# A decoder layer on one core: last-stage weights fetched in quarters, and three instruction orders changed around the attention heads and the last norm

## The reference

```python
x = x + attn(layernorm(x))                       # one head of width 128, Wqkv, Wo, biases
x = x + xattn(layernorm(x), ctx, mask, pos_bias) # 32 heads of width 128, with an RMS norm inside
x = x + ffn(layernorm(x))                        # below
# xattn, for each of 32 heads and 8 sequences
score = softmax(where(mask, h_q @ h_k.T + pos_bias, -inf)); attn = score @ h_v; out = attn @ w_out.T
# ffn
base = x @ base_W.T; probs = softmax(x @ router_W.T)            # 8 experts, the top 2 of them
mid = (x @ lora_A) * gates; out = base + 2 * (mid @ lora_B)     # rank 16 each
```

## Time and profile before

| what | value |
| --- | --- |
| median of 3 runs | 852.9 us (852.66 to 852.99) |
| the profiled execution, its own time | 854.52 us |
| span of its records | 852.8 us |
| granted clock of PE | 1.00 over the span |
| PE busy | 835.5 us, 98% |
| DVE busy | 643.3 us, 75% |
| ACT, POOL busy | 412.0 us and 361.7 us |

### The profile page before, as it was taken

One profiled execution on the slowest core, in us unless ns is written; L12 is line 12 of the kernel. 1 busy time (PEld: TensorE's weight loads), 2 busy tenths in 40 slices (PEclk: granted clock), 3 DMA queues, 4 the chain that ended last, 5 costly groups with the idle time before them and its releaser, 6 DMA issues.

```text
span 852.8 us, 14086 instructions
## 1 busy us (share of the span) xinstructions
PE 835.5 (98%) x4288; PEld 705.7 (83%) x4288; DVE 643.3 (75%) x1114; ACT 412.0 (48%) x1070; POOL 361.7 (42%) x332
## 2 busy tenths in 40 slices
PE   5999999999999999999999999999999999999998
PEld 4788888888778888878888888888888888888896
DVE  6988877788887876769867887778667876687754
ACT  3934445655554344365544555355534554454320
POOL 2413424324552333255466556553555455644000
PEclk9999999999999999999999999999999999999999
DMA  8026577657665568737966666576657675773002
GB/s 295 14 99 172 149 170 171 153 154 171 168 185 148 148 169 147 160 120 208 251 205 203 196 192 189 183 220 202 183 177 222 176 203 178 203 199 72 1 1 99
DMA packets 231282, 139.79 MB, mean 164 GB/s; under 512 B 139216, under 2 KB 205904, under 8 KB 229328
## 3 DMA queue, kind: packets, MB, share of 16 engines
q1 hardware_dynamic: 231248, 139.38, 60.2%
HBM read 90.07 MB, written 49.28 MB: 163 GB/s over the span
## 4 chain that ended last, share of the span: by engine, by line
PE 88%; DVE 5%; DMA 3%; ACT 1%; POOL 1%; SPq 1%; issue 1%; DVEq 0%; POOLq 0%
PE bank L654 73%; PE bank L714 7%; PE bank L805 6%; DMA values<-turned 1%; DMA by_blocks<-probs 1%; SPq L356 1%; DVE turned L1525 1%; PE bank L677 1%; DVE acc L1298 1%; DVE stats L1305 1%; DVE xt_lo L1353 0%; DMA acc<-in_x 0%; DMA probs_t<-by_blocks 0%; ACT w_hi L1077 0%; DVE acc L1785 0%
## 5 line engine op out<-in xcount | busy, mean ns | idle before, releaser
L1085 ACT COPY st<-bank 128x512 f32<-128x512 f32 x192 | 112.6, 586 | 227.1 <-PE bank L654 226.2
L654 PE MATMUL bank<-ctx_hi,w_hi 128*128 128x512 f32 x448 | 176.8, 395 | 0.9 <-ACT st L1085 0.5
L1431 DVE TENSOR_TENSOR st<-bank,st 128x512 f32<-128x512 f32 x144 | 99.5, 691 | 101.3 <-PE bank L654 96.8
L654 PE MATMUL bank<-ctx_hi,w_lo 128*128 128x512 f32 x448 | 174.5, 390 | 0.0
L654 PE MATMUL bank<-ctx_lo,w_hi 128*128 128x512 f32 x448 | 174.5, 389 | 0.0
L539 POOL TENSOR_TENSOR w_sum<-raw 128x256 f32<-128x256 f32 x48 | 40.1, 836 | 228.1 <-PE bank L654 197.2
L607 POOL TENSOR_TENSOR weighed<-probs,row_scale 128x512 f32<-128x512 f32 x60 | 65.7, 1100 | 118.7 <-DVE row_scale L1383 118.1
L654 PEld LDWEIGHTS bank<-ctx_hi,w_hi 128*128 128x128 f32 x448 | 84.1, 188 | 22.9 <-ACT st L1085 4.4
L654 PEld LDWEIGHTS bank<-ctx_hi,w_lo 128*128 128x128 f32 x448 | 84.1, 188 | 17.7
L654 PEld LDWEIGHTS bank<-ctx_lo,w_hi 128*128 128x128 f32 x448 | 84.2, 188 | 16.7
L1026 ACT ACTIVATE probs<-probs,neg_max 128x128 f32<-128x128 f32 x248 | 96.1, 391 | 0.1
(11 more groups left out here) (153 smaller groups left out, 1514.1 us busy)
## 6 DMA issues: line engine op xcount, KB each, us to landing
raw<-in_weights SPq DMA_DIRECT2D x128, 256.0 KB, 3.4
values<-turned SPq DMA_DIRECT2D x64, 256.0 KB, 4.4
v<-values SPq DMA_DIRECT2D x64, 256.0 KB, 4.8
by_blocks<-probs SPq DMA_DIRECT2D x30, 512.0 KB, 3.2
probs_t<-by_blocks SPq DMA_DIRECT2D x120, 128.0 KB, 2.8
keys<-st SPq DMA_DIRECT2D x14, 1024.0 KB, 4.8
st<-keys SPq DMA_DIRECT2D x28, 512.0 KB, 5.5
acc<-in_x SPq DMA_DIRECT2D x8, 256.0 KB, 6.3
```

What stands on the lines that cost most here:

```text
L654: ins = pe.matmul(out_ap, lhs[a], rhs[b], start=start and k == 0, stop=stop and k == n - 1, skip_group_check=again)
L1085: act.copy(to[:, i, j, :], (y, other, y, y)[which][:, :]).then_inc(act_took, 1)
L1431: dve.tensor_tensor(to[:, i, j, :], (other, y, other)[which][:, :], to[:, i, j, :], ALU.add).then_inc(dve_took, 1)
```

## The change

Four edits. The last stage's weights are fetched in quarters, each at the end of one of the first four `refill` calls, which are written out instead of one; `high_ffn` waits for the count of its own quarter. The two turns of the first head's blocks on DVE stand before the first two `take` calls of K1 instead of behind them. The last head's two halves of values are weighed together, before the output of blocks 0 to 3. The last norm's first half is made in two steps of two blocks: DVE adds, statistics and spreads, POOL roots, ACT and DVE normalisation are interleaved anew, and PE turns rows two blocks at a time (`turn_last_rows`), with a wait for blocks 4 and 5 ahead of chunk 2; of the splits on DVE the first stands ahead of the adds of blocks 6 and 7. `routed(0)` no longer waits for all adds.

```diff
@@ -453,13 +453,16 @@
             fetch_bias(2)
             sp.wait_ge(k_stored, 16 * (GROUPS - 2))
 
-            def fetch_ffn():
-                n = 0
+            def fetch_ffn(i):
+
+                quarter, n = ffn_cols // FFN_PARTS, 0
                 for src, width in ((w_base, KC * C), (w_routed, KC * ROUTED), (w_lora_b, C)):
-                    sp.dma_start(ffn_raw[:, n:n + width], src).then_inc(ffn_loaded, 16)
+                    lo, hi = max(n, quarter * i), min(n + width, quarter * (i + 1))
+                    if lo < hi:
+                        sp.dma_start(ffn_raw[:, lo:hi], src[:, lo - n:hi - n]).then_inc(ffn_loaded, 16)
                     n += width
 
-            def refill(g, first=False, ahead=2):
+            def refill(g, ffn_part=None, ahead=2):
 
                 load_keys(g + 1, 0)
                 sp.wait_ge(pv_done, 2 * PAIR * g + 2)
@@ -474,11 +477,12 @@
                 next_out(g + 1)
                 if ahead == 2:
                     fetch_bias(g + 2)
-                if first:
-                    fetch_ffn()
-
-            refill(1, first=True)
-            with sp.Fori(2, GROUPS - 2) as g:
+                if ffn_part is not None:
+                    fetch_ffn(ffn_part)
+
+            for g in range(1, 1 + FFN_PARTS):
+                refill(g, g - 1)
+            with sp.Fori(1 + FFN_PARTS, GROUPS - 2) as g:
                 refill(g)
             refill(GROUPS - 2, ahead=1)
 
@@ -640,8 +644,9 @@
             with pool.Fori(3 + FFN_PARTS, GROUPS - 1) as g:
                 pair(g)
             pair(GROUPS - 1, last=True)
-            root(2, half(0), spans(2, 0))
-            root(2, half(1), spans(2, 1))
+            root(2, slice(0, 2), 6)
+            root(2, slice(2, HALF), 7)
+            root(2, half(1), 8)
 
 
         @block.tensor
@@ -656,18 +661,29 @@
                         k += 1
                 return ins
 
+            def turn_last_rows():
+
+                for k in range(2):
+                    pe.wait_ge(rows_ready, 6 + k)
+                    pe.wait_ge(rows_ready_v, 2 + k)
+                    for c in range(KC):
+                        if k == 0 and c in (0, 2):
+
+                            pe.wait_ge(out_added, B * GROUPS + 4 + c)
+                        for b in (2 * k, 2 * k + 1):
+                            ins = pe.transpose(ROWS_T[2][c][:, cols(b)], rows[:, b, cols(c)], ident[:, :])
+                        if k == 1:
+                            ins.then_inc(rows_t_done, 1)
+
             def turn_rows(layer, i):
                 if i == 0 and layer:
-                    pe.wait_ge(out_added, (0, B, B * (GROUPS + 1) - HALF)[layer])
-                pe.wait_ge(rows_ready, spans(layer, i))
+                    pe.wait_ge(out_added, B)
+                pe.wait_ge(rows_ready, spans(layer, i) + (layer == 2))
                 if layer == 2:
-                    pe.wait_ge(rows_ready_v, i + 2)
+                    pe.wait_ge(rows_ready_v, 4)
                 elif layer == 0:
                     pe.wait_ge(rows_ready_v, 1)
                 for c in range(KC):
-                    if layer == 2 and i == 0 and c == 2:
-
-                        pe.wait_ge(out_added, B * (GROUPS + 1) - 2)
                     if i:
                         if layer == 1:
                             pe.wait_ge(x_rows_copied, c + 1)
@@ -920,20 +936,16 @@
 
                 turn_last_probs(1)
                 weigh_head_values(g, 0, last=True)
-                weigh_head_values(g, 1, (0,), last=True)
+                weigh_head_values(g, 1, last=True)
                 pe.wait_ge(wo_lo_ready, GROUPS)
                 pe.wait_ge(out_added, B * g + 6)
                 pe.wait_ge(scores_biased, 2 * HEADS + 2)
                 pe.wait_ge(ot_lo_ready, 2 * HEADS - 1)
                 for b in range(HALF):
-                    if b == 3:
-
-                        pe.wait_ge(probs_t1_copied, 1 + PAIR)
                     part(b, 0)
                 pe.wait_ge(ot_lo_ready, 2 * HEADS + 1)
                 for b in range(HALF):
                     part(b, 1).then_inc(out_done, 1)
-                weigh_head_values(g, 1, (1,), last=True)
                 for b in range(HALF, B):
                     if b >= 6:
                         pe.wait_ge(out_added, B * GROUPS + b - 6 + 1)
@@ -979,10 +991,10 @@
                     three_pass(BASE[t][:, :], [([s[:, 0, cols(b)] for s in ot], lora_b_s)],
                                start=False).then_inc(ffn_done, 1)
 
-            turn_rows(2, 0)
+            turn_last_rows()
             pe.wait_ge(ffn_lo_ready, FFN_PARTS)
+            routed(0)
             pe.wait_ge(out_added, B * (GROUPS + 1))
-            routed(0)
             base_out(0, (0,))
             turn_rows(2, 1)
             base_out(0, (1, 2, 3))
@@ -1011,8 +1023,8 @@
                     act.activation(tok_raw[OF_X][:, slot, c % 2, :], ROWS_T[1][c][:, :], ACT.Copy,
                                    scale=ln_w_cols[:, c:c + 1]).then_inc(x_rows_copied, 1)
 
-            def normalise(layer, i, some, last=True):
-                act.wait_ge(rstd_ready, spans(layer, i))
+            def normalise(layer, i, some, last=True, ready=None):
+                act.wait_ge(rstd_ready, ready or spans(layer, i))
                 for b in some:
                     scale = rstd_rms[:, b:b + 1] if layer == 1 else rstd[:, 0, b:b + 1]
                     ins = act.activation(rows[:, b, :], acc[:, b, :], ACT.Identity, scale=scale, bias=shift[:, b:b + 1])
@@ -1254,7 +1266,7 @@
                     then()
 
             def high_ffn(i):
-                act.wait_ge(ffn_loaded, 48)
+                act.wait_ge(ffn_loaded, 16 * (1, 2, 4, 6)[i])
                 at = cols(i, ffn_cols // FFN_PARTS)
                 act.copy(ffn[0][:, at], ffn_raw[:, at]).then_inc(ffn_hi_ready, 1)
 
@@ -1272,7 +1284,8 @@
             copy_last_probs(1)
             split_head_out(GROUPS - 1, 0)
             split_head_out(GROUPS - 1, 1, VO)
-            normalise(2, 0, (0, 1))
+            normalise(2, 0, (0,), ready=6)
+            normalise(2, 0, (2,), ready=7)
 
             def split_last_rows(i):
                 for c in range(KC):
@@ -1281,7 +1294,7 @@
                                    scale=1.0).then_inc(xt_hi_ready, 1)
 
             split_last_rows(0)
-            normalise(2, 1, (4, 5))
+            normalise(2, 1, (4, 5), ready=8)
             split_last_rows(1)
             for i in range(2):
                 act.wait_ge(logits_ready, i + 1)
@@ -1636,13 +1649,13 @@
                     maxima(j + 1, j, first_probs[j], i)
             row_scales(0, 0, 0)
             row_scales(0, 0, 1)
+
+            dve.wait_ge(product_done, SLOTS * K1 + PAIR)
+            turn_probs(0, 0, 0)
+            turn_probs(0, 0, 1)
             take(K1, 0, kt)
             low_for_queries(1, 0)
             take(K1, 1, kt)
-
-            dve.wait_ge(product_done, SLOTS * K1 + PAIR)
-            turn_probs(0, 0, 0)
-            turn_probs(0, 0, 1)
             take(K1, 2, kt)
             low_for_queries(1, 1)
             row_scales(0, 1, 0)
@@ -1700,33 +1713,41 @@
             pair(GROUPS - 1, last=True)
             copy_last_probs(1)
             split_head_out(GROUPS - 1, 0)
-            split_head_out(GROUPS - 1, 1, (0,), VO)
-
-            def normalise_last(i):
-                dve.wait_ge(rstd_ready, spans(2, i))
-                for b in range(HALF * i + HALF // 2, HALF * (i + 1)):
+            split_head_out(GROUPS - 1, 1, banks=VO)
+
+            def normalise_last(some, count):
+                dve.wait_ge(rstd_ready, count)
+                for b in some:
                     ins = dve.tensor_scalar(rows[:, b, :], acc[:, b, :], mean_var[:, b, 0:1], rstd[:, 0, b:b + 1],
                                             ALU.subtract, ALU.mult)
                 ins.then_inc(rows_ready_v, 1)
 
-            for b in range(HALF):
+            def add_last(b):
                 add_out(GROUPS, b, LAST_OUT)
-                if b:
-                    row_stats(2, b - 1)
-            row_stats(2, HALF - 1)
-            spreads(2, half(0))
-            split_head_out(GROUPS - 1, 1, (1,), VO)
-            normalise_last(0)
-            add_out(GROUPS, 4, LAST_OUT)
-            add_out(GROUPS, 5, LAST_OUT)
-            add_out(GROUPS, 6, LAST_OUT)
-            add_out(GROUPS, 7, LAST_OUT)
-            row_stats(2, 4)
-            split_rows(2, 0)
-            for b in (5, 6, 7):
+
+            add_last(0)
+            row_stats(2, 0)
+            add_last(1)
+            row_stats(2, 1)
+            add_last(2)
+            spreads(2, slice(0, 2))
+            row_stats(2, 2)
+            add_last(3)
+            normalise_last((1,), 6)
+            row_stats(2, 3)
+            spreads(2, slice(2, HALF))
+            add_last(4)
+            normalise_last((3,), 7)
+            add_last(5)
+            split_rows(2, 0, (0,))
+            add_last(6)
+            split_rows(2, 0, (1,))
+            add_last(7)
```

(4 more changed lines are left out.)

## The result

The changed kernel's median is 856.14 us (852.51 to 859.65, 22 runs), that of the kernel before, over as many runs, 852.87 us (852.07 to 855.02). The ratio of the two is 1.0036, with a 95% interval of 1.0022 to 1.005: slower by 3.1 us, where I forecast 1.1 us less, and outside my range. The spread has grown from 3 to 7 us, and the runs fall in two groups by PE's mean granted clock over the execution. Ten have 1.000 and took 852.51 to 854.72 us (median 854.0). Twelve have 0.994 or 0.996 and took 855.94 to 859.65 us. The profiled execution is the slowest of the second group: span 857.9 us, clock 0.994.

The account below looks back on a forecast made before the run. PE, busy for 98% of the span, was taken as the bound; 852.8 - 1.68 (quarters) - 0.8 (early turns) + 1.35 (tail) = 851.7 us of span, 851.8 us as median; range for 8 in 10: 850.2 to 853.2.

Parts of the forecast that it names:

- The tail at full clock: Last head's end to last stage: joined halves and two-step norm together lose 1.35 us, bounds 0.5 and 2.0.
- The first root: POOL's root in the last norm: ready at 802.5, so DVE's first normalisation does not wait.
- both of DVE's idle spells: Last norm: DVE idles 0.6 us before the second normalisation and 1.6 us before the first split.
- Rival (a): Tail: adds of blocks 6 and 7 slip into DVE's idle time; 0.5 lost to 1.0 gained, 849.4 to 850.9 us; chance 0.2.
- Quarters: Pair 2 among the heads: splitting the weight fetch removes the whole stall and slow restart, 1.68 us gained.
- the limit of 6.56: Among the heads: time in us from a store's issue to the load's issue before PE stalls.
- Rival (c): Pairs 2 to 5: each quarter delays its store past the limit, so four pairs stall; 855.8 us, two pairs 853.8; chance 0.08.
- Early turns: First head's block turns on DVE: start at about 365.9, the first weighing's stall and slow restart go, 0.8 us gained.
- slot 5: PE's slot waiting for the first take, now behind the turns: a stall of 0.1 and a restart of 0.1.
- rival (b): Early turns bring nothing because pair 1 or slot 5 gives the 0.8 back; 852.6 us; chance 0.1.

Follow-up runs that it names:

- e12: Kernel before with the two tail edits alone (halves together, norm in two steps), without quarters and early turns; 858.04 us, ratio 1.0049.
- e11: The changed kernel, unchanged, run for a second profile; 856.61 us.
- e1: Kernel before with the quarters and early turns alone, heads' end and last norm as before; 852.87 us, ratio 0.9992.
- e2: Kernel before with quarters, early turns and the last head's halves weighed together, norm in one step as before; 853.62 us, ratio 1.0004.
- e6: Kernel before with the quarters alone; 853.00 us, ratio 0.9999.
- e7: Kernel before with the early block turns alone; 852.71 us, ratio 0.9995.
- e5: Kernel before, unchanged, for a second profile; span 851.7 us.
- e8: Changed kernel with unread matmuls in PE's tail waits: 4 ahead of chunk 2, then 3, 1, 1 ahead of the last stage's first chunks; 854.21 us, ratio 1.0012.
- e9: Changed kernel with DVE's order mended and three unread matmuls on PE ahead of the last stage's first chunk; 851.64 us, ratio 0.9978.
- e4: Changed kernel with 24 unread matmuls in PE's tail waits (8 ahead of chunk 2, then 8, 4, 4); 856.42 us, ratio 1.0031.
- e10: Changed kernel with DVE's order mended and the last head's fourth half weighed late again, as before the change; 852.73 us, ratio 0.9988.
- e3: Changed kernel with DVE's adds of block 5 ahead of the second normalisation, of 6 and 7 ahead of the first split; 852.47 us, ratio 0.9989.

## Why the prediction was wrong, point by point

**The clock** is the step that is missing. I worked out the waits of PE (of the size that was measured), and priced each at its own length. Nothing in the sum, the rivals or the range had the granted clock in it, since the page of before showed 1.00 throughout. The mean clock was 0.994 or 0.996 in 12 of 22 executions and in 9 of 12 in e12, and the three profiles of such executions (the first, e11, e12) show a fall to 0.50 for seven to ten us, at 3.2 to 4.8 us each. In the kernels with the old norm (e1, e2, e6, e7) the mean was 0.999 or 1.000 in all 45; in the kernel before it was 0.994 in one of the 30 runs beside e5 to e8 and one of the 17 beside e12, and 0.998, with 856.94 us, in one of the 21 beside e9 to e11. With PE's waits filled, it was low in none of 19 (e4, e8). So that PE stands idle there is shown as the cause, by e8 above all, whose real work starts at the same moments. What in the idling does it isn't shown. It isn't the total alone, since e2 idles for as long in two waits and fell in none of eleven; and four waits aren't needed, since e10 fell after one. Nor is it shown why some executions fall and others of the same kernel don't: all three profiles of this tail are of executions that fell, so none shows what the others do differently. The Trainium skill (TensorE: Matmul & The Clock Gate, section A second HAM failure mode: psum-queue depth-cycling) tells of a kernel whose clock swings because PE idles briefly, but often, between groups of matmuls. The trace of the changed kernel agrees in kind: no gap was longer than 1.0 us, but four lay close together. The kernel before, with two gaps of 0.62 and 0.73 around longer bursts, mostly stays clear. e10's single gap of 0.85 doesn't fit that picture, and here the measurement decides.

**The tail at full clock** was right: I said 1.35 us, e8 shows 1.32. By its parts, the joined halves cost 0.89 with the norm in one step, and the norm in two steps 0.43 (e2 to e8); with DVE's order mended the join costs 0.1 at most by e10. The first root was ready when DVE came, and both of DVE's idle spells stand where I put them. Rival (a) is refuted for the order as written and true for the mended order: e3's tail gains 0.44.

**Quarters**: the mechanism was right and the price wrong. I took 1.68 us from the one profiled execution. Store to load was 8.12 in that one and 6.16 in the next, on either side of the limit of 6.56 that I had worked out; the four profiles with the whole fetch have 8.12, 6.93, 6.16 and 6.12, and stalls of 1.4, 0.2 and none. e6 shows a gain of 0.1 in the ratio, interval from 0.9 gained to 0.7 lost. The profiled execution was itself 1.65 us over the median (854.52 against 852.87), which I noted and then set differences from its span on the median. Rival (c) is refuted: quarters give 3.0 to 4.4 us in pairs 2 to 5 of all ten profiles that have them, never near 6.56.

**Early turns**: turns at 365.94 for my 365.9, the gap before the first weighing gone, and a gap of 0.06 at slot 5 by e7's chain. At that place the 0.8 that I counted is gained; how much of it reaches the end is less clear. In e7's profile 0.4 to 0.5 comes back in pair 2, not in the pair 1 that rival (b) names, and the ratio of e7 says 0.4 gained (1.1 gained to 0.3 lost), which excludes neither my 0.8 nor rival (b).

**Sum as measured.** Quarters and turns 0.7 gained (e1, 0 to 1.5), tail 1.32 lost (e8): 0.6 more than before at full clock, where the ten such executions show 1.1, a difference that e1's interval covers; and 3.2 to 4.8 us on top in over half of the executions, which moves the median to 3.3 over. So the clock isn't the only miss: even at full clock 854.0 lies over my upper bound of 853.2, because the two edits among the heads, priced at 2.48 together, gave 0.7.

## What to carry to other kernels

Work out not only how long the engine that bounds the kernel will wait, but how often in close succession: short waits between short bursts can cost the clock, at more than their own length (2.4 us of waits, and 3.2 to 4.8 us on top where the clock fell), and in part of the executions only, so look at the granted clock of each run and at the spread as well as at the median. Before pricing a stall by one profile, set that execution's own time against the runs; a stall that hangs on how long a store takes behind a fetch, near its limit, may be absent in the median one. And put work that is ready into an engine's known idle spells, in front of the instruction that waits, not behind it: moving three adds that way turned the two-step norm from a loss of 0.43 us into a gain of 1.33.

## What the runs showed of the hardware that I had not expected

PE's granted clock fell to 0.50 with no wait longer than 1.0 us ahead of it, in e10 with a single one of 0.85, and stayed there for seven to ten us of unbroken matmuls. A `pe.matmul` on plain float32 operands of 128 x 120 columns is two PE instructions, 0.22 us in all (e4). From the issue of a 0.5 MB store with a 1.5 MB fetch ahead of it to that of the load that waits for it were 8.1 us in one execution of the kernel before and 6.2 in another.
